# A two-layer decoder kernel: the first batches of its self attention placed among the last groups of the cross attention, their scales worked out by group and by half

## What is computed

```python
x = x + tanh(g_xattn[0]) * L0_xattn(layernorm(x), ctx, ctx)   # Q K V, softmax over 4 keys a head, Wo
x = x + tanh(g_ffn[0]) * L0_ffn(layernorm(x))
def L0_ffn(X):
    h = X * rsqrt(mean(X * X) + 1e-6) * norm1_w
    q, k, v = h @ wq, h @ wk, h @ wv                          # 16 heads of 8
    X = X + softmax(q k^T / sqrt(8)) v @ wo                   # 128 x 128 scores a head
    ...                                                       # router, top 2 of 8 experts, shared expert
x = x + tanh(g_xattn[1]) * L1_xattn(layernorm(x), ctx)
x = x + tanh(g_ffn[1]) * L1_ffn(layernorm(x))
```

## Time and profile before

| what | value |
|---|---|
| median of 3 runs | 529.53 us (529.13 to 532.28) |
| the profiled execution | 529.87 us, its span 528.1 us |
| mean granted TensorE clock in it | 0.961 |
| busy: TensorE, VectorE, ScalarE, GpSimd | 465.9, 379.5, 268.6, 311.0 us |
| projections of batches 0 to 5 (L1651) begin at | 48.4, 53.2, 58.0, 63.3, 74.7, 83.9 us |
| projection of batch 15 begins at | 152.5 us, 0.09 us a batch over the beat of 6.77 |
| projection of a batch at full clock; T (L1038); values apart (L1046) | 0.84; 0.48; 0.34 us |
| `attend` at full clock and at half clock | 1.4 and 2.50 us |
| X (L991); KT (L1054); row maximum (L1022) | 0.75; 0.69; 0.65 to 0.69 us |
| `probabilities` (three instructions) | 1.55 us |
| a step of the splits on GpSimd; a piece of halves | 0.40 to 0.48; 1.15 us |
| `scales_of_half(0)` and `(1)` | 7.7 us from 38.33; 7.4 us from 61.90 |
| clearing of one KS; tgb (L1219) | 0.64; 0.28 us |
| loads issued behind `halved` | at 96.57, 123.59, 156.81 us |
| first matmul of the experts | at 184.61 us |

### The profile page before, as it was taken

How to read it: one execution, slowest core, us unless ns; L and a number is a source line. 1 busy time by engine, 2 the same in 40 slices (tenths; PEclk the granted TensorE clock), 3 DMA queues, 4 the chain that set the end, 5 groups by cost and what they waited for, 6 DMA issues and landing times.

```text
span 528.1 us, 10878 instructions
## 1 busy us (share of the span) xinstructions
PE 465.9 (88%) x3679; PEld 347.3 (66%) x3702; DVE 379.5 (72%) x960; ACT 268.6 (51%) x505; POOL 311.0 (59%) x509
## 2 busy tenths in 40 slices
PE   3768869999999689869998989899989997988895
PEld 2646546777667468657776867587757765766673
DVE  5463647889998587987775788668976797667753
ACT  2231347777777456445457335644465447433452
POOL 6866787888964065526753466347635663354453
PEclk9996769999999899989999999999999999898999
DMA  6510000301001002000000000000000000000000
GB/s 161 135 63 0 2 1 2 113 2 53 3 11 45 2 1 51 1 0 1 1 1 1 2 0 2 0 0 0 0 0 2 0 1 20 2 1 21 0 20 22
DMA packets 19339, 9.81 MB, mean 19 GB/s; under 512 B 6520, under 2 KB 18777, under 8 KB 19289
## 3 DMA queue, kind: packets, MB, share of 16 engines
q1 hardware_dynamic: 17848, 8.84, 6.1%
q10 hardware_dynamic: 1440, 0.33, 0.3%
HBM read 8.12 MB, written 1.05 MB: 17 GB/s over the span
## 4 chain that ended last, share of the span: by engine, by line
PE 54%; DVE 19%; POOL 10%; issue 9%; ACT 4%; DMA 2%; SPq 1%; POOLq 0%; another core or an unknown queue 0%; DVEq 0%; ACTq 0%
PE PS L1746 9%; PE PS L1747 8%; PE PS L1748 8%; POOL HLO L583 4%; PE PS L1611 3%; PE PS L1617 3%; DVE work L1297 3%; PE PS L1606 3%; PE PS L1579 2%; PE PS L1651 2%; DMA X<-in_x_dram 2%; POOL grstd L600 2%; PE PS L1594 2%; DVE work L1302 1%; PE PS L1801 1%
## 5 line engine op out<-in xcount | busy, mean ns | idle before, releaser
L583 POOL TENSOR_TENSOR HLO<-work,HHI 128x512 fp32r<-128x512 f32 x112 | 144.7, 1294 | 139.4 <-ACT HHI L803 135.7
L810 ACT ACTIVATE work<-PS 128x512 f32<-128x512 f32 x112 | 66.9, 597 | 100.0 <-PE PS L1748 96.3
L1297 DVE TENSOR_TENSOR work<-work,PS 128x512 f32<-128x512 f32 x104 | 70.9, 682 | 50.2 <-ACT work L810 19.9
L803 ACT ACTIVATE HHI<-work 128x512 fp32r<-128x512 f32 x111 | 69.8, 629 | 42.2 <-DVE work L1302 42.1
L1302 DVE TENSOR_TENSOR work<-PS,work 128x512 f32<-128x512 f32 x112 | 77.1, 691 | 15.2 <-POOL HLO L583 6.2
L1022 DVE TENSOR_REDUCE nmax<-PS 128x4 f32<-128x512 f32 x64 | 42.3, 682 | 7.9 <-PE PS L1579 7.6
L697 ACT ACTIVATE EX<-PS 128x512 f32<-128x512 f32 x64 | 34.9, 605 | 13.5 <-PE PS L1594 13.4
L1746 PE MATMUL PS<-HHI,W0H_down 128*128 128x512 f32 x72 | 34.9, 485 | 0.2
L1746 PE MATMUL PS<-H2H,W0H_gate 128*128 128x512 f32 (+1 forms) x72 | 32.3, 449 | 1.5 <-issue 0.8
L1746 PE MATMUL PS<-H2H,W0H_up 128*128 128x512 f32 (+1 forms) x72 | 29.7, 412 | 2.9 <-DVE work L1302 2.9
L1747 PE MATMUL PS<-H2L,W0H_up 128*128 128x512 f32 (+1 forms) x72 | 28.6, 398 | 0.0
(11 more groups left out here) (355 smaller groups left out, 1210.4 us busy)
## 6 DMA issues: line engine op xcount, KB each, us to landing
X<-in_x_dram SPq DMA_DIRECT2D x4, 256.0 KB, 8.1
raw<-in_L_ffn_e_gate_dram SPq DMA_DIRECT2D x1, 1024.0 KB, 5.5
raw<-in_L_ffn_e_up_dram SPq DMA_DIRECT2D x1, 1024.0 KB, 7.7
out_dram<-X SPq DMA_DIRECT2D x4, 256.0 KB, 2.3
ctx_nat<-in_ctx_dram SPq DMA_DIRECT2D x2, 308.0 KB
raw<-in_L_ffn_We_gate_dram SPq DMA_DIRECT2D x1, 512.0 KB, 3.8
raw<-in_L_ffn_We_up_dram SPq DMA_DIRECT2D x1, 512.0 KB, 3.8
raw<-in_L_ffn_We_down_dram SPq DMA_DIRECT2D x1, 512.0 KB, 4.1
```

The source lines that it names most:

```text
L583: pool.tensor_tensor(HLO[t][:], HH[k % 2][:], HHI[t][:].bitcast(F32), ALU.subtract).then_inc(m_sem["lo"], 1)
L803: act.activation(HHI[turn_of(m, g, k)][:], HH[k % 2][:], ACT.Copy).then_inc(S["hi"], 1)
L810: act.activation(SG[c % 2][:], PS[:, c % 2, :], ACT.Silu).then_inc(S["silu"], 1)
L1297: dve.tensor_tensor(SG[c % 2][:], SG[c % 2][:], PS[:, 4, :], ALU.mult).then_inc(S["scaled"], 1)
```

## The change

1. GpSimd works out the scales of the first half by group (`scales_of_group`), each as soon as its group's moments are there. VectorE makes mean and variance out of the statistics with a new instruction for each batch (`bn_aggr`, in `attended`), into `topf`, which is free until the router.
2. VectorE works out the scales of the second half (`second_half_scales`), behind slot -2, with the seed and three steps of Newton's method; GpSimd waits for its signal `sc` at batch 8.
3. Batches 0 to 2 of the self attention are placed among groups 2 and 3 of the cross attention, on TensorE, VectorE and ScalarE; of 16 idle transpositions 4 are left.
4. GpSimd clears KS ahead of its first scales and the other tiles after batch 1's Z. The halves of weights come two batches later.

```diff
@@ -102 @@
+        amoments = topf
@@ -418 @@ GpSimd
-            def scales_of_half(k):
-                at = slice(k * HALF, (k + 1) * HALF)
-                pool.wait_ge(a_sem["st"], 2 * k + 2)
-                moments(at, HALF)
...
-                inverse_root(rs2[:, k].rearrange("p a b -> p (a b)"), var2[:, k].rearrange("p a b -> p (a b)"), p_d[:])
...
+            def scales_of_group(g):
+                at = slice(g * GB, (g + 1) * GB)
+                v, r = var2[:, 0, :, at], rs2[:, 0, :, at]
+                t = p_d[:, 0:2 * GB].rearrange("p (a b) -> p a b", a=2)
+                pool.wait_ge(a_sem["mv"], g + 1)
+                pool.tensor_scalar(mean[:, at], amoments[:, at, 0], -1.0, None, ALU.mult)
+                pool.tensor_scalar(v[:, 0, :], amoments[:, at, 1], LN_EPS, None, ALU.add)
+                step(pool.tensor_scalar(v[:, 1, :], amoments[:, at, 1], 1.0 + RMS_EPS, LN_EPS * RMS_EPS, ALU.mult, ALU.add))
+                step(pool.tensor_tensor(r, v, less_half[:].unsqueeze(1).broadcast_to([P, 2, GB]), ALU.pow))
...
@@ -447,457 @@ (BB, CS and bm are cleared after batch 1's Z instead)
+            for u in range(NKS):
+                step(pool.memset(KS[u][:].bitcast(F32), 0.0))
+                step(pool.memset(KS[u][:, :, 48:50], 1.0))
+            pool.sem_inc(consts, 1)
             first_scales(1, G)
@@ -494 @@
+                if b == HALF:
+                    pool.wait_ge(a_sem["sc"], 1)
@@ -516 @@
-                for k, c in pieces[b * per_batch:(b + 1) * per_batch]:
+                for k, c in pieces[max(b - 2, 0) * per_batch:max(b - 1, 0) * per_batch]:
@@ -535 @@
-            scales_of_half(0)
-            batches(slot, -3, 1)
-            scales_of_half(1)
-            batches(slot, 1, B)
+            scales_of_group(0)
+            batches(slot, -3, -1)
+            pool.memset(BB[:], 0.0)
+            step(pool.memset(CS[:].bitcast(F32), 0.0))
+            step(pool.memset(bm[:], 0.0))
+            batches(slot, -1, 0)
+            scales_of_group(1)
+            batches(slot, 0, B)
@@ -687,783 @@ ScalarE
-            turned_group(3)
             act.wait_ge(small_in, 16 * 7)
+            turned_input(0)
+            turned_group(3)
+            high_keys(0)
+            turned_input(1)
             turned_probabilities(2)
+            high_queries(0)
             exp_group(3)
-            batches(slot, -4, -2)
+            high_keys(1)
+            turned_input(2)
+            turned_queries(0)
             turned_probabilities(3)
-            batches(slot, -2, B)
+            high_queries(1)
+            high_keys(2)
+            batches(slot, -1, B)
@@ -994 @@ VectorE, attended(g)
+                dve.wait_ge(a_sem["st"], g + 1)
+                for j in range(GB):
+                    ins = dve.bn_aggr(amoments[:, g * GB + j, :], stats[:, g * GB + j, :])
+                ins.then_inc(a_sem["mv"], 1)
@@ -1010,1206 @@
-            probabilities(2)
-            less_row_maximum(3)
-            attended(2)
+            def second_half_scales():
+                v, r, at = var2[:, 1].rearrange("p a b -> p (a b)"), rs2[:, 1].rearrange("p a b -> p (a b)"), slice(HALF, B)
+                t, c = t_b[:], t_c[:, 0:HALF]
+                dve.wait_ge(a_sem["mv"], G)
+                dve.tensor_scalar(var2[:, 1, 0, :], amoments[:, at, 1], LN_EPS, None, ALU.add)
+                lnc(dve.tensor_scalar(var2[:, 1, 1, :], amoments[:, at, 1], 1.0 + RMS_EPS, LN_EPS * RMS_EPS, ALU.mult, ALU.add))
+                lnc(dve.tensor_scalar(r.bitcast(I32), v.bitcast(I32), -0.5, RSQRT_SEED, ALU.mult, ALU.add))
+                for _ in range(3):
+                    lnc(dve.scalar_tensor_tensor(out=t, in0=r, scalar=-0.5, in1=r, op0=ALU.mult, op1=ALU.mult))
+                    lnc(dve.tensor_tensor(t, t, v, ALU.mult))
+                    lnc(dve.scalar_tensor_tensor(out=r, in0=t, scalar=1.5, in1=r, op0=ALU.add, op1=ALU.mult))
...
+                dve.sem_inc(a_sem["sc"], 1)
             queries_and_keys(0)
             values_apart(0)
-            probabilities(3)
+            probabilities(2)
+            less_row_maximum(3)
             queries_and_keys(1)
             values_apart(1)
+            attended(2)
             turned_keys(0)
+            probabilities(3)
+            queries_and_keys(2)
             attended(3)
-            queries_and_keys(2)
             batches(slot, -3, -1)
+            second_half_scales()
@@ -1556,1725 @@ TensorE
-            turn_group(3)
-            turn_probabilities(2)
-            strided_scores(3)
-            attend(2)
-            keep_going(4, PS[:, 4, 0:P])
...
-            batches(slot, -6, -5)
-            pe.wait_ge(a_sem["xt"], G)
-            keep_going(6, PS[:, 7, 2 * P:3 * P])
-            batches(slot, -5, -4)
-            turn_probabilities(3)
-            keep_going(6, PS[:, 7, 2 * P:3 * P])
-            batches(slot, -4, -3)
+            turn_input(0)
+            turn_group(3)
+            pe.wait_ge(a_sem["v2_sb"], G)
+            keep_going(4, PS[:, 0, 0:P])
+            project(0)
+            strided_scores(3)
+            turn_input(1)
+            turn_probabilities(2)
+            project(1)
+            attend(2)
+            turn_keys(0)
+            turn_input(2)
+            turn_queries(0)
+            turn_probabilities(3)
             attend(3)
             batches(slot, -3, B)
```

More of the change, by code:

```diff
@@ L419, in first_scales @@
                 step(pool.tensor_tensor(nmr[:, at], mean[:, at], rstd[:, at], ALU.mult))
-            def scales_of_half(k):
-                at = slice(k * HALF, (k + 1) * HALF)
-                pool.wait_ge(a_sem["st"], 2 * k + 2)
-                moments(at, HALF)
-                pool.tensor_scalar(var2[:, k, 0, :], var[:, at], LN_EPS, None, ALU.add)
-                step(pool.tensor_scalar(var2[:, k, 1, :], var[:, at], 1.0 + RMS_EPS, LN_EPS * RMS_EPS, ALU.mult, ALU.add))
-                inverse_root(rs2[:, k].rearrange("p a b -> p (a b)"), var2[:, k].rearrange("p a b -> p (a b)"), p_d[:])
-                pool.tensor_tensor(nmr[:, at], mean[:, at], rs2[:, k, 0, :], ALU.mult)
-                step(pool.tensor_tensor(p_a[:, 0:HALF], var2[:, k, 0, :], rs2[:, k, 0, :], ALU.mult))
-                step(pool.tensor_tensor(r2[:, at], p_a[:, 0:HALF], rs2[:, k, 1, :], ALU.mult))
+            def scales_of_group(g):
[7 more added lines that the diff above has]
+                step(pool.tensor_tensor(r, v, less_half[:].unsqueeze(1).broadcast_to([P, 2, GB]), ALU.pow))
+                step(pool.tensor_tensor(t, r, r, ALU.mult))
+                step(pool.tensor_tensor(t, t, v, ALU.mult))
+                step(pool.tensor_scalar(t, t, -0.5, 1.5, ALU.mult, ALU.add))
+                step(pool.tensor_tensor(r, r, t, ALU.mult))
+                pool.tensor_tensor(nmr[:, at], mean[:, at], r[:, 0, :], ALU.mult)
+                step(pool.tensor_tensor(p_a[:, 0:GB], v[:, 0, :], r[:, 0, :], ALU.mult))
+                step(pool.tensor_tensor(r2[:, at], p_a[:, 0:GB], r[:, 1, :], ALU.mult))
             def normalised_group(g):
@@ L459, in _ @@
                 bias_group(g)
-            pool.memset(BB[:], 0.0)
-            for u in range(NKS):
-                step(pool.memset(KS[u][:].bitcast(F32), 0.0))
-                pool.memset(KS[u][:, :, 48:50], 1.0)
-            step(pool.memset(CS[:].bitcast(F32), 0.0))
-            pool.memset(bm[:], 0.0).then_inc(consts, 1)
             def clear_selectors():
@@ L1012, in _ @@
             attended(1)
-            probabilities(2)
-            less_row_maximum(3)
-            attended(2)
-            dve.wait_ge(consts, 2)
             def row_maximum(b, j):
@@ L1207, in slot @@
                     difference_of_two(0)
+            def second_half_scales():
[9 more added lines that the diff above has]
+                    lnc(dve.scalar_tensor_tensor(out=r, in0=t, scalar=1.5, in1=r, op0=ALU.add, op1=ALU.mult))
+                dve.scalar_tensor_tensor(out=nmr[:, at], in0=amoments[:, at, 0], scalar=-1.0, in1=rs2[:, 1, 0, :], op0=ALU.mult, op1=ALU.mult)
+                lnc(dve.tensor_tensor(c, var2[:, 1, 0, :], rs2[:, 1, 0, :], ALU.mult))
+                lnc(dve.tensor_tensor(r2[:, at], c, rs2[:, 1, 1, :], ALU.mult))
+                dve.sem_inc(a_sem["sc"], 1)
+            dve.wait_ge(consts, 2)
             queries_and_keys(0)
             values_apart(0)
-            probabilities(3)
+            probabilities(2)
+            less_row_maximum(3)
             queries_and_keys(1)
             values_apart(1)
+            attended(2)
             turned_keys(0)
+            probabilities(3)
+            queries_and_keys(2)
             attended(3)
-            queries_and_keys(2)
             batches(slot, -3, -1)
+            second_half_scales()
             dve.wait_ge(small_in, 16 * 7)
```

2 lines of the change are left out of this document (1 added, 1 removed).

## The result

Twenty executions of the changed kernel have a median of 528.82 us (521.47 to 534.35), twenty of the kernel before 529.15 (526.47 to 534.74). These medians are 0.33 us apart, and the means of all twenty 1.5 us. The ratio given for the change is 0.9943, 95% interval 0.9917 to 0.9969, about 3.0 us won, within 1%; this ratio, and those of the table further on, are of the fast executions alone, those within 1.5% of the fastest of their kernel, which leaves out the seven slowest of after's twenty (529.33 us and more) and one of before's (534.74). The profiled execution took 525.28 us, against 529.87. So there are two things to explain: 4.6 us between the profiles, and why so much less is left over twenty executions.

The account below looks back on a forecast made before the run. TensorE's self-attention loop bounds the kernel from 83.94 us, 6.77 us a batch; only the stretch ahead changes. 83.94 − 78.0 − 1.0 = 4.9 us won; 529.87 − 4.9 − 0.34 gives 524.6 us, range 520.3 to 528.6.

Parts of the forecast that it names:

- 1: Z of batch 0: GpSimd's scales of group 0 alone take 4.5 us, so Z of batch 0 begins at 36.9 instead of 46.06 us.
- 2: projections 0 and 1: TensorE's projections of batches 0 and 1 come at about 39.0 and 42.7 us, before at 48.4 and 53.2.
- 3: stop for `probabilities(3)`; projection 2: TensorE stands 3.1 us while VectorE finishes `probabilities(3)`; projection 2 at 52.0 to 53.0, 5 to 6 us won.
- 4: projection 2 to third scores; projection 3: VectorE's work behind projection 2 delays batch 0's third scores 4.3 us, before 2.81; projection 3 between 58.8 and 60.8.
- 5: projection 3 to 4; projection 4: With the second half's scales off GpSimd, this slot takes 6 us instead of 11.4; projection 4 between 64.3 and 67.3.
- 6: 15 steps on VectorE: Second half's scales on VectorE, ahead of batch 2's row maxima: 0.25 us a step, 3.8 us, upper bound 5.5.
- 7: projection 4 to 5; projection 5: TensorE's slot takes 10.2 us at full clock, up to 3 more at 1.2 GHz; projection 5 at 78.0.
- 8: stop; cost beyond projection 5: TensorE stands about 3.3 us ahead of batch 2's third scores; the lowered clock costs 1.0 us beyond projection 5.
- The first rival: TensorE stays at 2.4 GHz and GpSimd disturbs nothing: projection 5 at about 74, 9.9 us won, 519.6 us; chance 0.19.
- What I cost at nothing: Covered by idle time: KS memsets (1.9 us uncovered), group 1's scales (4.5), later weight pieces (3.5), later loads, `sc` wait.
- The clock that stays down: Ten microseconds at 1.2 GHz behind the stop for batch 2's third scores: 2.0 us won, 527.5 us; chance 0.19.
- The slower rival: GpSimd's shifted pieces collide with VectorE's two-input instructions in the loop, up to 0.57 us each; chance 0.08, over 1% 0.04.

Follow-up runs that it names:

- busy: Changed kernel with TensorE turning an identity 24 and 28 times in its two long waits; median 520.7 us, ratio to before 0.9837.
- second profile of after: The changed kernel, unchanged, profiled once more; 529.59 us.
- halves_back: Changed kernel with GpSimd splitting the weights' pieces in their old slots again, not two batches later; median 529.7 us, ratio to before 0.9992.
- alone: Kernel before with only bn_aggr on VectorE and GpSimd's scales by group for groups 0 and 1; median 532.1 us, ratio to before 1.0051.
- gp_groups: Changed kernel with the scales of the third and fourth group back on GpSimd, by group, in its waits; median 522.2 us, ratio to before 0.9867.

## Why the prediction was right, and where not

The forecast (3 to 7 us won, within 1% of no change) holds: 4.6 us in the profile, and 3.0 by the ratio, at its lower end; 0.9943 × 529.53 is 526.5 us, and the point, 524.6, is 1.9 us low. Over all twenty executions less was won, 1.5 us by the means and 0.3 by the medians, so part of the agreement is luck: the forecast has one time for a kernel whose executions lie 13 us apart. Its steps against the profiled execution of after:

| step | forecast | measured |
|---|---|---|
| 1: Z of batch 0 | 36.9 | 36.43 |
| 2: projections 0 and 1 | 39.0, 42.7 | 38.98, 43.27 |
| 3: stop for `probabilities(3)`; projection 2 | 3.1; 52 to 53 | 3.19; 53.37 |
| 4: projection 2 to third scores; projection 3 | 4.3; 58.8 to 60.8 | 4.78; 61.62 |
| 5: projection 3 to 4; projection 4 | 6 (5.4 to 6.9); 64.3 to 67.3 | 6.37; 67.99 |
| 6: 15 steps on VectorE | 3.8 | 3.81 |
| 7: projection 4 to 5; projection 5 | 10.2 to 13.2; 78.0 | 12.04; 80.03 |
| 8: stop; cost beyond projection 5 | 3.3; 1.0 | 3.73; none |

- *The durations and the waits were right.* Steps 1, 2, 5 and 6 and both stops, who ends them and how long they last, came out of the old rows within 0.6 us.
- *The term that was mis-sized is the clock between 48 and 66 us*, in steps 3 and 4. I let `attend(3)` run at 1.2 GHz at most; all the work up to 65.5 did. Projections 2 and 3 took 1.65 us each instead of 0.91, the turns 1.03 instead of 0.62. Of the 2.0 us by which projection 5 missed 78.0, 0.6 was there at projection 1, ahead of this stretch, and 1.2 more by projection 3. `busy` shows a part of this to be the clock and not a wait: it leaves the stops and gains 1.7 us up to projection 4. Between projections 2 and 3 no run of after's order has the full clock throughout, so that part is read from the durations alone.
- *I read the clock of the kernel before wrongly.* I took two stretches at 1.2 GHz into account and wrote that stops of about 1 us leave the clock alone. There were four; the two others, 3.4 us each, began at 53.1 us, behind stops of 0.96 and 1.20 us, and at 63.3, behind one of 1.49. From the windows of before:
```profile
54.00:56.00 2.00, 1.97 (x14) 1.38 (x13) 1.36 (x3) 0.94 (x3) 0.56 (x2) 0.50 0.00 0
...
64.00:66.00 2.00, 2.00 (x16) 0.93 (x15) 1.50 (x5) 0.51 (x2) 1.85 (x3) 0.50 0.00 0
```
The first rival rested on short stops that leave the clock at 2.4 GHz, and steps 3 and 4 allow next to nothing for it. Between 34 and 92 us TensorE was at 1.2 GHz for 27.3 us before and for 27.4 in the first profile of after: the change moved that time, it added none.
- *Two errors cancelled.* 3.84 us were won at projection 5, not 5.9. The charge of 1.0 beyond it was not due (80.03 to 86.80 is a beat), and 0.69 was won behind projection 15, where before had the clock at 0.50 from 179.4 to 182.8 us and after did not: 3.84 + 0.06 in the loop + 0.69 = 4.6.
- *Step 6 has a spread.* In the second profile of after the 15 steps took 4.6 us (71.74 to 76.35), in `halves_back` 4.5: two-input steps of 0.17 us took 0.58 to 0.69 beside the subtractions of GpSimd's pieces. That is inside 2.9 to 5.5. The 8 us which the rule of the Trainium skill ("SBUF — State Buffer", "Who interferes with whom") would have given, with each step waiting, came in no run; that some steps take three times as long agrees with it.
- *What I cost at nothing.* The later pieces cost nothing where I could compare them at one clock (`halves_back`), and over all executions their shift may even be what wins. With the memsets moved, GpSimd began the scales of group 0 at 31.70, 0.3 us behind the last aggregation. But I had taken for granted that moving the second half to VectorE is paid by the stop it makes (3.73). `alone` and `gp_groups` put the other side: on GpSimd, too late, the same scales make TensorE stop for 2.75 (before) and 4.93 us, and in its waits for nothing.
- *The rivals.* The clock that holds (519.6) did not come in any run of after, though five of 26 executions took 521.5 to 522.9. The clock that stays down (527.5) describes the median better than my forecast, but for another stop: the long stretch began with the first stop and not behind VectorE's scales, where it lasted 3.4 us. The trace agrees with the Trainium skill ("TensorE: Matmul & The Clock Gate", "Part 1: The HAM clock gate") that idling brings the clock down; it shows that a TensorE busy for 12.88 of 16.80 us stayed at 1.2 GHz. The slower rival did not come: from projection 5 to 15 went 68.56 us, before 68.62.

## What to carry to other kernels

When a change makes the next stage start earlier, walk the new order engine by engine and look for the first engine that runs out: here two new stops of over 3 us each came from the order of VectorE's program, and another order took both away. A chain of small steps that nobody needs soon belongs in the idle time of several beats, or on an engine that waits anyway, not in front of a value that TensorE waits for. And where TensorE stops at the start of a kernel, measure more than one execution: the stop can be paid twice, once as time and once as a clock that differs from one execution to the next, and turning an identity meanwhile is a cheap test of the second part (3.2 us in the pair of profiles here).
